# An attention and mixture-of-experts layer on one core: relay through memory in runs of 64 floats, next scores ahead of the transposes, gate behind the first tile of keys

## The reference

```python
q = (layernorm(x) @ Wq.T).reshape(B, N, 16, 16)
k, v = (ctx @ Wk.T), (ctx @ Wv.T)              # same shape: 16 heads of 16 channels
attn = softmax(einsum('bnhd,bngd->bnhg', q, k) / 4)   # over g: heads against heads, token by token
a = einsum('bnhg,bngd->bnhd', attn, v)
x = x + transpose(a, (0, 2, 1, 3)).reshape(B, N, C) @ Wp.T + bp
y = layernorm(x)
x = x + sum over the 2 best of 16 experts (gate logits y @ gate_w.T) + shared SwiGLU feed-forward of y
```

## Time and profile before

| | us |
|---|---|
| median of 3 runs | 1795.53 |
| lowest and highest run | 1794.02, 1797.23 |
| profiled execution, device time | 1800.4 |
| its span in the trace | 1798.6 |
| TensorE matmuls busy | 1513.8 (84%) |
| VectorE busy | 1326.2 (74%) |
| GpSimd busy | 1315.4 (73%) |
| ScalarE busy | 726.7 (40%) |

### The profile page before, as it was taken

How to read it: one execution, slowest core, us unless ns; L and a number is a source line. 1 busy time by engine, 2 the same in 40 slices (tenths; PEclk the granted TensorE clock), 3 DMA queues, 4 the chain that set the end, 5 groups by cost and what they waited for, 6 DMA issues and landing times.

```text
span 1798.6 us, 50791 instructions
## 1 busy us (share of the span) xinstructions
PE 1513.8 (84%) x17109; PEld 1320.3 (73%) x17110; DVE 1326.2 (74%) x3378; ACT 726.7 (40%) x1346; POOL 1315.4 (73%) x1253
## 2 busy tenths in 40 slices
PE   4699999999999999999999999976677676676774
PEld 4578888888878887888888888855566666665774
DVE  6677889787999899988998999875455555455553
ACT  3344454445444544454445444422133332233231
POOL 4277787778787877878787878767567777677676
PEclk9799999999999999999999999987788988889887
DMA  8788888888898889888988898845877765777773
GB/s 219 151 191 174 175 164 228 184 181 164 212 199 173 173 207 199 176 175 182 224 176 178 186 212 175 151 166 210 259 216 215 223 210 165 216 210 228 210 216 91
DMA packets 945835, 344.76 MB, mean 192 GB/s; under 512 B 824088, under 2 KB 898730, under 8 KB 940288
## 3 DMA queue, kind: packets, MB, share of 16 engines
q1 hardware_dynamic: 892464, 166.19, 51.7%
q0 software_dynamic: 33600, 92.91, 14.0%
q10 hardware_dynamic: 19728, 85.13, 13.0%
HBM read 200.37 MB, written 148.15 MB: 194 GB/s over the span
## 4 chain that ended last, share of the span: by engine, by line
PE 31%; issue 17%; SPq 16%; DVE 13%; another core or an unknown queue 7%; POOL 6%; DMA 5%; ACT 4%; DVEq 0%; POOLq 0%; ACTq 0%
SPq L276 6%; SPq L281 5%; SPq L289 4%; PE bank_z L1460 4%; PE bank_a L1193 3%; PE bank_y L1180 2%; PE bank_y L1178 2%; PE bank_a L1332 2%; PE bank_y L1179 2%; ACT xn L645 2%; PE bank_z L1178 2%; DMA w_sb<-q_dram 2%; DMA kv_dram<-w_sb 2%; PE bank_z L1180 2%
## 5 line engine op out<-in xcount | busy, mean ns | idle before, releaser
L410 POOL DMA_INDIRECT slots<-xn,slot_i x256 | 279.4, 1091 | 98.2 <-issue 55.0
L1132 DVE SCALAR_TENSOR_TENSOR v_area<-bank_y,tail,v_area 128x256 f32<-128x256 f32 x288 | 121.6, 478 | 155.6 <-PE bank_y L1180 68.2
L531 POOL DMA_INDIRECT sums<-v_area,tail x144 | 147.1, 1022 | 65.3 <-issue 33.5
L1178 PE MATMUL bank_y<-w_hi,xn_hi 128*128 x288 | 98.8, 343 | 110.9 <-POOL xn_lo L523 79.6
L531 POOL DMA_INDIRECT out<-v_area,tail x144 | 147.5, 1024 | 52.9 <-issue 35.6
L722 ACT ACTIVATE th<-bank_z 128x512 f32<-128x512 f32 x72 | 43.0, 598 | 297.5 <-PE bank_z L1460 141.1
L1178 PEld LDWEIGHTS bank_y<-w_hi,xn_hi 128*128 128x128 f32 x288 | 59.5, 206 | 127.6 <-issue 127.2
L419 POOL DMA_INDIRECT sums<-v_area,slot_i x128 | 128.1, 1000 | 33.2 <-issue 29.8
L1178 PE MATMUL bank_y<-wsh_out_hi,hid_hi 128*128 128x256 f32 x512 | 143.0, 279 | 1.3 <-POOL hid_lo L441 1.3
L1180 PE MATMUL bank_y<-wsh_out_hi,hid_lo 128*128 128x256 f32 x512 | 142.8, 279 | 0.0
L1179 PE MATMUL bank_y<-wsh_out_lo,hid_hi 128*128 128x256 f32 x512 | 142.7, 279 | 0.0
(11 more groups left out here) (229 smaller groups left out, 5381.1 us busy)
## 6 DMA issues: line engine op xcount, KB each, us to landing
k_area<-slots SPq DMA_DIRECT2D x288, 129.0 KB
v_area<-sums SPq DMA_DIRECT2D x288, 128.0 KB
kv_dram<-w_sb ACTq DMA_DIRECT2D x32, 1024.0 KB
x_sb<-in_x_in SPq DMA_DIRECT2D x32, 512.0 KB
ctx_sb<-in_ctx_t SPq DMA_DIRECT2D x32, 512.0 KB
q_dram<-q_sb ACTq DMA_DIRECT2D x32, 512.0 KB
k_area<-kv_dram SPq DMA_DIRECT2D x256, 64.0 KB
w_sb<-q_dram SPq DMA_DIRECT2D x256, 64.0 KB
```

Of the source, the lines that this page charges most:

```text
L410: pool.indirect_dma_start(slots[j], bass.IndirectOffsetOnAxis(ap=slot_i[:, par, j, i:i + 1], axis=0), row_of[j][:, i, :], None).then_inc(S ...
L531: pool.indirect_dma_start(target, bass.IndirectOffsetOnAxis(ap=tail[:, r, t, 1 - j:2 - j].bitcast(u32), axis=0), y_ring[:, r, t, :], None, ...
L1132: st = nc.vector.scalar_tensor_tensor(out=y_ring[:, r, t, :], in0=Y[t // 2][:, t % 2 * C:(t % 2 + 1) * C], scalar=tail[:, r, t, j:j + 1], ...
L1178: mm(out, lhs_hi, rhs_hi, start=start, stop=False)
```

## The change

**The relay in runs of 64 floats.** Token tile i now holds every fourth token instead of 128 in a row, so a partition holds four neighbours. The q and k rows are kept in SBUF with the four tiles side by side, and stored by eighths in four DMAs each, of 32 partitions; v has a DRAM tensor and one store of its own. The 24 reads of a chunk then have runs of 64 floats. For this TensorE's stationary operands in `project` are taken with a step of four floats (`slice(i, TOK, BPC)`), those of the scores too (`q_by_row`), and ScalarE writes q with that step. The load of `x_in` becomes four DMAs of 32 partitions.

**TensorE's order.** `body(c)` begins with `scores(c)`, then `turn(c - 1)`, then the first tile of keys, then `gate(c - 1)`, then the rest of `project`. The scores wait in addition for VectorE's residual of the chunk before (`h2_ready`), whose banks they overwrite.

```diff
-        q_rows = w2_sb[:, BPC * 2 * C:].rearrange("p (m h) -> p m h", h=32)
+        q_rows = w2_sb[:, BPC * 2 * C:].rearrange("p (n c f) -> p n c f", c=2, f=BPC * H)
+        q_by_row = w2_sb[:, BPC * 2 * C:].rearrange("p (n f i) -> p n i f", i=BPC, f=2 * H)
-                sp.wait_ge(S["kv_stored"], at(16, c, 16))
+                sp.wait_ge(S["kv_stored"], at(80, c, 80))
-                    sp.dma_start(k_diag[rows, :, t % 4, :],
-                                 kv[src, :, :, 0, :].rearrange("n i (d g) -> d (n i) g", d=D)).then_inc(S["qk_read"], 16)
+                    sp.dma_start(k_diag[rows, t % 4, :, :].rearrange("d (n a) g -> d n (a g)", a=BPC), k[src]).then_inc(S["qk_read"], 16)
+            def store_by_eighth(dram, rows, done):
+                by_i = dram.rearrange("(t i n) f -> i t n f", t=8, i=BPC)
+                for i in range(BPC):
+                    act.dma_start(by_i[i], rows[32 * i:32 * i + 32, :]).then_inc(S[done], 16)
-                act.dma_start(kv_dram[c], kv_sb).then_inc(S["kv_stored"], 16)
+                store_by_eighth(k_dram[c], kv_sb[:, 0:BPC * C], "kv_stored")
+                act.dma_start(v_dram[c], kv_sb[:, BPC * C:]).then_inc(S["kv_stored"], 16)
-                        st = nc.scalar.activation(q_sb[:, t, :], Q_BANKS[i][:, j * C:(j + 1) * C], ACT.Copy, scale=ln1_rstd[:, t:t + 1])
+                        st = nc.scalar.activation(q_by_tile[:, t], Q_BANKS[i][:, j * C:(j + 1) * C], ACT.Copy, scale=ln1_rstd[:, t:t + 1])
...
             def scores(c, first):
                 pe.wait_ge(S["qk_read"], at(256, c, 256))
+                if not first:
+                    pe.wait_ge(S["h2_ready"], at(2, c, 0))
...
-                            last = mm(SCORE_BANKS[u][32 * a:32 * a + 32, n * 4 * H:(n + 1) * 4 * H], q_rows[:, m, :],
-                                      k_diag[:, m, :, :].rearrange("p t g -> p (t g)"), start=True, stop=True)
+                            last = mm(SCORE_BANKS[u][32 * a:32 * a + 32, n * 4 * H:(n + 1) * 4 * H], q_by_row[:, row, tile, :],
+                                      k_diag[:, :, m, :], start=True, stop=True)
...
-                        tokens = slice(i * P, (i + 1) * P)
+                        tokens = slice(i, TOK, BPC)
                         last = mm_split(KV_BANKS[i][:, :], ctx_hi[:, k, tokens], ctx_lo[:, k, tokens],
                                         wkv_hi[:, k, :], wkv_lo[:, k, :], k == 0, k == KT - 1)
                     last.then_inc(S["kv_full"], 1)
+                    if gate_of is not None and i == 0:
+                        gate(gate_of)
...
             def body(c, first, ahead):
                 scores(c, False)
-                gate(c - 1)
+                turn(c - 1)
                 if ahead:
-                    project(c + 1, False, True, first)
+                    project(c + 1, False, True, first, c - 1)
+                else:
+                    gate(c - 1)
...
                 shared_down(c - 1, first)
-                turn(c)
```

More of the change, by code:

```diff
@@ L258, in _, with load_x_in @@
         def _(sp):
+            def load_x_in(c):
+                rows = x_in[c].rearrange("(m t) i f -> i m t f", t=BPC)
+                for i in range(BPC):
+                    sp.dma_start(x_sb[32 * i:32 * i + 32, :, :], rows[i]).then_inc(S["x_in_done"], 16)
             def chunk(c, first, last):
@@ L261, in chunk @@
                     sp.wait_ge(S["ln1_step"], at(1, c, 1))
-                    sp.dma_start(x_sb[:, :, :], x_in[c + 1]).then_inc(S["x_in_done"], 16)
+                    load_x_in(c + 1)
                     sp.wait_ge(S["ctx_split"], at(1, c, 1))
@@ L288, in chunk @@
                         r = QUARTER_OF[i] * 2 + t2
[L289 to L292 removed]
+                        sp.dma_start(v_diag[16 * r:16 * r + 16, r % 4, :, :].rearrange("g (m i) d -> g m (i d)", i=BPC),
+                                     v[i, t2]).then_inc(S["v_read"], 16)
+            load_x_in(0)
             sp.dma_start(wq_sb, wq).then_inc(S["w_q"], 16)
@@ L1191, in scores @@
                         for a in range(4):
-                            m = (u * 8 + n) * BPC + QUARTER_OF[a]
-                            last = mm(SCORE_BANKS[u][32 * a:32 * a + 32, n * 4 * H:(n + 1) * 4 * H], q_rows[:, m, :],
-                                      k_diag[:, m, :, :].rearrange("p t g -> p (t g)"), start=True, stop=True)
+                            row, tile = QUARTER_OF[a] * 4 + u * 2 + n // 4, n % 4
+                            m = row * BPC + tile
+                            last = mm(SCORE_BANKS[u][32 * a:32 * a + 32, n * 4 * H:(n + 1) * 4 * H], q_by_row[:, row, tile, :],
+                                      k_diag[:, :, m, :], start=True, stop=True)
                     last.then_inc(S["s_full"], 1)
@@ L1205, in gate, with project @@
                 last.then_inc(S["g_full"], 1)
-            def project(c, first, gated, ranks_first=None):
+            def project(c, first, gated, ranks_first=None, gate_of=None):
                 if first:
@@ L1333, in attend @@
                                       prob_t[:, 32 * g:32 * g + 32],
-                                      v_diag[:, pair * 16 + u * 8 + n, :, :].rearrange("p t d -> p (t d)"), start=True, stop=True)
+                                      v_diag[:, :, pair * 16 + u * 8 + n, :], start=True, stop=True)
                     last.then_inc(S["o_full"], 1)
@@ L1412, in _ @@
             c = CHUNKS - 1
+            turn(c)
             gate(c)
```

45 lines of the change are left out of this document (22 added, 23 removed).

## The result

The changed kernel takes 1956.06 us (median of 4 runs, 1948.64 to 1968.90) beside 1795.49 for the kernel before, a ratio of 1.0895 with an interval of 1.0859 to 1.0931. That is slower, as forecast, but by 160 us where 60 were forecast, and outside the range of 1800 to 1892. The loss lies in the chunks. The queries' copies of two neighbouring chunks stand 36.3 us apart before, and 41.7 after (means of 20 chunks). That is 5.4 us a chunk, some 165 us in 31 chunks, so the whole loss.

The account below looks back on a forecast made before the run. The prediction took TensorE and the pair VectorE with GpSimd as near the bound. Profiled 1800.4 + 70 (order and strided queries) - 10 (relay and start) = 1860.4, less 4.9 to the median: 1855.5 us, range 1800 to 1892.

Parts of the forecast that it names:

- TensorE's order alone: TensorE's new order in each chunk: L834 ends later behind GpSimd's subtractions, about 1.05 us a chunk lost, 31 us.
- the rest of 70: Chunk loss of 2.33 us, 30 x 2.33 = 70 us, the order's 1.05 included; the remainder is the queries' slower strided loads.
- nine stores on ScalarE: ScalarE's stores in each chunk: 7 more issues at 0.37 us, 2.6 us, claimed to cost nothing.
- relay in time, start: Scores' DMA waits shrink, 3.5 us saved; earlier scores and v at the kernel's start save 6.5; 10 us once.
- The far end given: ScalarE's stores ahead of the first tanh: 1.1 us a chunk if that delay were uncovered.
- the row of L855: VectorE operation starting inside a GpSimd scatter, ending only behind the next GpSimd operation; taken as evidence that L834 waits for both.
- VectorE gets in between: Rival: L834 is served between x_split and xn_lo; 1816 us with slow loads (chance 0.07), 1742.5 with free loads (0.14).
- the scores' loads: TensorE's strided loads in the scores: 0 taken; rival with up to a doubling, 54 us more, 1909.5 us, chance 0.08.
- relay isn't faster: Rival: stores of 32 partitions spread badly, scores wait at least 1.88 us; 1911 us, or 1872 with free loads; chance 0.05.

## Why the prediction was wrong

The forecast was 1855.5 us. The kernels with one half each, and those with a cause taken away, give the terms. From the kernel before to the changed one they add up along one path: relay, step, stores, order, 3 + 57 + 92 + 11 = 163 us, where 160 were measured.

| term | forecast, us | measured, us | from |
|---|---|---|---|
| TensorE's order alone | +31 | +34 | order alone, 1827.04 |
| the order on top of the relay | in the sum | +11 | 1956.06 against 1945.46 |
| the order, stores on SyncE | | +24 with the step, +199 without | 1877.29 and 1852.90; 1995.79 and 1796.33 |
| operands with a step | +39 (the rest of 70) | +57 in the old order | 1852.90 against 1796.33 |
| nine stores on ScalarE | 0 | +92 old order, +79 new | 1945.46 and 1852.90; 1956.06 and 1877.29 |
| relay in time, start | -10 | +3, within its error | 1796.33 against 1793.10 |

The order and the step have no price of their own that holds in every kernel; the rows show how much the price depends on the rest. The sum for the start has a slip of 0.2 us (1.5, 3.2 and 2 are 6.7, not 6.5), which changes nothing.

**The step that failed** is in the relay's part: "ScalarE issues nine stores instead of two, 7 x 0.37 = 2.6 us", and "They cost nothing: three of them delay the first tanh (638.80) by 1.1 us". Three things were wrong in it. The issue was priced by the row of a whole store, and a store of 32 partitions takes 0.8 us: nine take 6.6 us, where the two of before take 0.74. The queue was followed to the tanh only, but `load_res` stands behind the same stores. And it wasn't asked who waits for that load: VectorE's bias_add, then the turns of the attention sum, then TensorE's output projection. The far end given, 1.1 us a chunk, was the price of the wrong wait. The stores cost 79 us in the new order and 92 in the old one, and the load moved ahead of them alone gives back 75. Without this term the changed kernel takes 1877 us, which lies inside the stated range.

**The order.** Right by number, wrong by mechanism. The prediction took L834 to be starved by x_split and xn_lo, by the row of L855. It is served in between in every kernel with the new order: 747.75 + 1.19 = 748.94 after, where x_split ends at 748.91 and xn_lo starts at 748.88. The rival "VectorE gets in between" had the right mechanism and the wrong end: less than a microsecond later `hot` (749.56) ran into xn_lo and ended at 751.41 with it, so the gain was taken back by the same engine in the same chunk. The page SBUF — State Buffer of the Trainium skill, Who interferes with whom, says that the second to issue blocks until the first finishes. It says so of VectorE's two-port modes, and of a `tensor_tensor` with both inputs in SBUF that it contends with GpSimd's reads. L848 and L853 here agree with such a block, and L855 before and L880 after don't: L880 starts inside a scatter (754.04 to 755.00), the next GpSimd operation (755.03 to 756.10) goes first, and L880 ends only at 756.13, as the prediction read L855. So the row of L855 was read rightly; it didn't carry over from a scatter to a subtraction, and why is open. The transposes take 1.09 us with no wait, as forecast (1.10). Ranks wait 0.4 us with the order alone, forecast 1.3. Of the 34 us the larger part are the waits for q and for `hot`; the first belongs to the old relay, so the prediction, which adds the order to the new one, couldn't have it. That 31 and 34 lie close is luck.

**The strided operands.** The step was right and its size near: 2.45 us a chunk was taken from VectorE's rows, the far end was 2.8. The queries' matmuls come 0.237 us apart (754.65 to 757.25, eleven steps) where they came 0.117 apart, so 2.9 us a chunk, the far end. Advanced Engine Details and Errata of the Trainium skill, SBUF Cachelines, which spoke against this edit, is borne out: the load of 128 columns takes 332 ns with the step and 188 without. In time it costs 1.8 us a chunk in the old order. In the changed kernel taking it away gave nothing back (1962.79 against 1956.06), and in the new order with SyncE's stores it was 118 us worse, both beside holds. For the scores' loads 0 was taken, and they cost 0.4 us a chunk (743.62 - 741.42 = 2.20 against 1.82).

**The relay.** Confirmed in its aim: no DMA wait before the scores after, 36.4% of the queue instead of 51.7%. It bought nothing: its waits were 10.1 us in all, and the scores' slower loads, 0.4 us in each of 31 chunks, take as much (worked out, not measured apart). The rival "relay isn't faster" priced something else, late reads, and missed the stores too.

## What to carry to other kernels

When one transfer is cut in several, price the issue by a row of the same shape, and follow everything that stands behind it on that queue to whoever waits for it; a load that somebody waits for can be issued ahead of stores that nobody is in a hurry for. A strided operand of TensorE is free only while its load hides: here it hid behind 512 columns and not behind 256. And a part that is made faster can meet another engine's work at a worse moment; take both ends of a change apart before believing a sum.

## What the runs showed that was not expected

**Engines can stand still beside GpSimd's scatters.** Two kinds were seen. ScalarE starts long after the matmul that it waits for: 741.67 to 750.71, 7.5 us or more in 19 of 20 chunks, with TensorE running on. And TensorE starts the small matmuls of the attention sum in groups 0.7 us apart, 8.2 us instead of 2.5. Both went with the scatters when these were moved: the first from 8.3 us behind the matmul (median) to 3.4 and to nothing, the second came when five scatters stood beside the attention sum. A wait of GpSimd between the fourth and the fifth scatter took 150 us off the kernel. Shown is that the scatters' places matter. They aren't enough: the changed kernel and the one with the order alone also have eight scatters beside the queries (with 0.4 us between the fourth and the fifth), and there the copies start within 0.1 and 1.1 us of their matmuls. In the kernel before the two rows of four have 1.28 us of idle time between them. Not shown is the mechanism: a late signal, a late instruction of the waiting engine, or both. A kernel without the scatters was not tried.

**A faster operand made the kernel slower.** With SyncE's stores and the new order, the step of four floats took 1877 us and operands in a row 1996. The faster queries put their second copy into the hold, TensorE then waited 107.1 us in 20 chunks in front of the third `shared_z`, and its granted clock from 300 to 1200 us was 0.92 of full speed, where it was 1.00.

**An issue's price goes with its shape**: 0.37 us for a store of 128 partitions, 0.81 for one of 32, on ScalarE.
